# Moving the two copies of a head's row maxima from SP's DMA queue to ACT's

## The reference

```
q, k, v = x @ Wq, x @ Wk, x @ Wv          # 16 query heads of 32; layer 0: 4 key heads with rope
att = einsum('bhqd,bhkd->bhqk', q, k) / sqrt(32)
att = softmax(where(causal, att, -inf))
y   = einsum('bhqk,bhkd->bhqd', att, v)
x   = x + y @ Wo
```

## Time and profile before

| | |
|---|---|
| median of 3 runs | 2565.97 us (2558.61 to 2567.2) |
| time of the profiled execution | 2561.6 us |
| its span | 2559.9 us |
| mean granted TensorE clock | 0.993 |
| PE busy | 96% of the span |
| DVE, ACT, POOL busy | 68%, 50%, 59% |
| chain that ended last | PE 81%, DVE 6%, POOL 3%, ACT 2%, issue 2%, DMA 1%, SP's queue 1% |

### The profile page before, as it was taken

One profiled execution on the slowest core, in us unless ns is written; L12 is line 12 of the kernel. 1 busy time (PEld: TensorE's weight loads), 2 busy tenths in 40 slices (PEclk: granted clock), 3 DMA queues, 4 the chain that ended last, 5 costly groups with the idle time before them and its releaser, 6 DMA issues.

```text
span 2559.9 us, 45686 instructions
## 1 busy us (share of the span) xinstructions
PE 2451.0 (96%) x16544; PEld 1938.2 (76%) x16544; DVE 1751.9 (68%) x3608; ACT 1285.7 (50%) x2521; POOL 1509.2 (59%) x2045
## 2 busy tenths in 40 slices
PE   6999989999999999899999999999999889999999
PEld 4788767676768888688888888776777578888887
DVE  7788579979976344756565555788588866565555
ACT  6555346646664223554555443566466645454443
POOL 5433567667662334876677643666456876676662
PEclk9999999999999999999999999999999999999999
DMA  4222032122221110111111113233233211111112
GB/s 152 74 75 71 33 82 52 47 68 56 56 57 50 38 54 1 39 61 50 50 50 50 50 41 75 72 89 73 53 89 86 58 54 50 50 50 56 59 60 74
DMA packets 85840, 154.01 MB, mean 60 GB/s; under 512 B 17264, under 2 KB 26480, under 8 KB 85616
## 3 DMA queue, kind: packets, MB, share of 16 engines
q1 hardware_dynamic: 85616, 151.09, 20.5%
HBM read 87.58 MB, written 13.63 MB: 40 GB/s over the span
## 4 chain that ended last, share of the span: by engine, by line
PE 81%; DVE 6%; POOL 3%; ACT 2%; issue 2%; DMA 1%; SPq 1%; DVEq 0%; POOLq 0%; ACTq 0%
PE psum L1393 41%; PE psum L1444 23%; PE psum L1539 5%; PE psum L1502 5%; PE psum L1520 4%; PE psum L1550 2%; DVE psum L1972 2%; PE psum L1402 1%; ACT s4a1e L1757 1%; DVE s1a0rden L2011 1%; SPq L2251 1%; POOL s1a0e L2166 1%; ACT s1a0e L1757 1%; POOL s4a1e L2166 0%; POOL x L2174 0%
## 5 line engine op out<-in xcount | busy, mean ns | idle before, releaser
L1972 DVE CUSTOM_DVE_ANT_0 psum<-psum,mask_q 128x512 f32<-128x512 f32 (+5 forms) x768 | 413.1, 574 | 97.8 <-PE psum L1502 94.8
L1925 DVE SCALAR_TENSOR_TENSOR x<-psum,x 128x512 f32<-128x512 f32 x256 | 176.7, 691 | 289.6 <-PE psum L1393 289.2
L1757 ACT ACTIVATE s4a1e<-psum,p_scale 128x384 f32<-128x384 f32 (+5 forms) x384 | 206.1, 580 | 93.2 <-PE psum L1520 89.6
L1757 ACT ACTIVATE s1a0e<-psum,p_scale 128x384 f32<-128x384 f32 (+5 forms) x384 | 202.4, 578 | 79.7 <-PE psum L1520 78.3
L1393 PE MATMUL psum<-s5f1wd,s5f1a 128*128 128x512 f32 x768 | 196.7, 393 | 3.0 <-DVE s5f1a L1917 2.2
L1444 PE MATMUL psum<-s3f1h,wmem 128*128 128x512 f32 x768 | 195.3, 397 | 3.4 <-DVE s3f1h L1886 2.2
L1393 PE MATMUL psum<-s3f1wd,s3f1a 128*128 128x512 f32 x768 | 198.1, 393 | 0.3 <-issue 0.3
L1444 PE MATMUL psum<-s5f1h,wmem 128*128 128x512 f32 x768 | 192.6, 394 | 0.0
L2166 POOL TENSOR_TENSOR s4a1e<-s4a1e 128x896 f32<-128x896 f32 (+3 forms) x128 | 164.8, 1287 | 17.5 <-ACT s4a1e L1757 6.6
L2166 POOL TENSOR_TENSOR s1a0e<-s1a0e 128x896 f32<-128x896 f32 (+3 forms) x128 | 164.5, 1285 | 17.1 <-ACT s1a0e L1757 5.8
L1444 PEld LDWEIGHTS psum<-s3f1h,wmem 128*128 128x128 f32 x768 | 143.4, 188 | 38.0 <-issue 4.6
(11 more groups left out here) (233 smaller groups left out, 6186.5 us busy)
## 6 DMA issues: line engine op xcount, KB each, us to landing
raw<-in_down SPq DMA_DIRECT2D x76, 256.0 KB, 3.9
s1a0qst<-s1a0qs SPq DMA_DIRECT2D x96, 128.0 KB, 2.4
s4a1qst<-s4a1qs SPq DMA_DIRECT2D x96, 128.0 KB, 2.4
s4a1kst<-s4a1ks SPq DMA_DIRECT2D x96, 128.0 KB, 2.4
s3f1graw<-in_gate SPq DMA_DIRECT2D x32, 256.0 KB, 3.0
s3f1graw<-in_up SPq DMA_DIRECT2D x32, 256.0 KB, 3.1
s5f1graw<-in_gate SPq DMA_DIRECT2D x32, 256.0 KB, 3.0
s5f1graw<-in_up SPq DMA_DIRECT2D x32, 256.0 KB, 3.0
```

What stands on the lines that cost most here:

```text
L1757: act.activation(T[s]["e32"][:, begin_ + z * pw:begin_ + (z + 1) * pw - skip], src, ACT.Exp, bias=p_scale[:]).then_inc(sem["exp"], 1)
L1925: dve.scalar_tensor_tensor(x[:, tile, :], src, 0.5, x[:, tile, :], ALU.mult, ALU.add).then_inc(sem["x_add"], 1)
L1972: dve.tensor_tensor_reduce(scores, scores, mask_q[:, first:first + pw], -1.0, -MASKED, ALU.add, ALU.min, T[s]["negmax"][n % 2][:, column:c ...
```

## The change

The function that waits for the two parts and issues the two copies is taken out of SP's program and put into ACT's, under the same step (`m_lo`) of the same plan. The plan, the tiles, the semaphores and the copies themselves stay as they are; PSUM banks too.

```diff
 in scalar_program:
+            def m_move(s, n):
+                t, j = T[s], n % HPG
+                ready = (("m_hi", "m_hi"), ("m_lo", "m_lo"))
+                for p, (name, kind) in enumerate(ready):
+                    dst = t["qst"][STACK + p:STACK + p + 1, j, :].bitcast(F32)
+                    on.wait_ge(sem[name], at(name, kind, s, n))
+                    act.dma_start(dst.rearrange("o (i q) -> o i q", q=P),
+                                 t["mrow"][n % 2][p][:].bitcast(F32)).then_inc(m_in[n % 2], 16)
...
-                     "key": key, "y_hi": y_hi}
+                     "key": key, "y_hi": y_hi, "m_lo": m_move}
 in sync_program:
-            def m_lo(s, n):
-                t, j = T[s], n % HPG
-                ready = (("m_hi", "m_hi"), ("m_lo", "m_lo"))
-                for p, (name, kind) in enumerate(ready):
-                    dst = t["qst"][STACK + p:STACK + p + 1, j, :].bitcast(F32)
-                    on.wait_ge(sem[name], at(name, kind, s, n))
-                    sp.dma_start(dst.rearrange("o (i q) -> o i q", q=P),
-                                 t["mrow"][n % 2][p][:].bitcast(F32)).then_inc(m_in[n % 2], 16)
...
-                     "w_back": w_back, "stack": stack, "m_lo": m_lo}
+                     "w_back": w_back, "stack": stack}
```

## The result

| | before | after |
|---|---|---|
| median of 20 runs each | 2564.53 us (2558.61 to 2572.96) | 2570.96 us (2566.96 to 2577.53) |
| ratio of after to before | | 1.0027, interval 1.0017 to 1.0037 |
| time of the profiled execution | 2561.6 us | 2576.6 us |
| its span | 2559.9 us | 2574.9 us |
| mean granted TensorE clock | 0.993 | 0.988 |

A forecast was written before the change was run, and what follows sets the result against it. PE was taken to bound the kernel, busy 96% of the span and 81% of the chain. Terms +14.5 + 1.5 - 4.0 = +12 us on the median 2565.97 gave 2578 us, range 2562 to 2596.

The forecast's parts named there:

- the likeliest case: Both runs of heads: ACT issues of 0.65 us overlapping the running exp, net +6 to +18 us; chance 0.45.
- The walk through the heads: All 64 heads: each delayed exp followed to the matmul taking its bank; 17 heads lose 0.3 to 1.5 us, sum 14.5.
- The copies were hidden already: In 45 of 64 heads SP already waited for `m_hi`, so copies mostly begin no earlier; head 16's landed 0.6 us early.
- the faster rival: SP's queue: earlier stacks, weights and `y` copies remove most DMA waits, 4.9 - 13 = -8 us, 2558; chance 0.07.
- The rival in series: ACT's queue: each issue waits until the running exp is over, +26 us, 2592; chance 0.18.
- the rival of a very short issue: ACT's issue takes 0.1 to 0.3 us, or PE's idle time or existing waits cover losses: +1 us, 2567; chance 0.27.
- The second exp 0.84 us late in head 16: Head 16 of a0: the 384-column exp starts behind the second issue, 0.84 us late; PE loses about 0.07 us.
- Sum of PE's loss: PE waiting for late exps: 14.5 us over 64 heads, 4.9 with 0.1 us issues, 27 with 0.9 us.
- meeting SP: ACT issues beside SP's in 19 of 64 heads: 1.5 us taken, bounds nothing to 4 us.
- SP gives back 4 us: a1, heads 3 and 23: earlier copy and output weight shorten PE's waits, 4 us taken, range 0 to 6.
- The mutual holding: ACT and SP issuers hold each other: 0.9 us and more per issue, in series, over +35 us; chance 0.03.
- PE's idle time grows by 15 us: Profile sign: PE's waits for ACT's exps grow in both attentions by about 15 us.

The follow-up runs named there:

- SP held back: The kernel after, with SP still waiting for DVE's low part as before and issuing nothing there: 2573.60 us, 1.0026 of the kernel before.
- the wait alone: The kernel before, with ACT also waiting for DVE's low part and issuing nothing, SP keeping both copies: 2564.76 us, 1.0003 of the kernel before.
- twice the issues: The kernel after, with a second 4 KB DMA to unread DRAM scratch behind each copy on ACT: 2616.11 us, 1.0190 of the kernel before.
- the early output weight: The kernel before, with the output weight's load put three units earlier on SP: 2564.11 us, 0.9990; once more 2563.40 us, 0.9990.

## Why the prediction was right, and what was mis-sized

The forecast was 2578 us with 2562 to 2596; 2570.96 lies inside that range, just below the likeliest case's own 2572 to 2584. The mechanism came out as it was told, in the part of its chance (0.12 of 0.45) that was to stay below +0.3%; the size is little more than half of the forecast. The walk through the heads is on record in two of them only, 16 and 27, so its sums can be held against measured totals but not redone head by head. The range's upper end, 2596, is not the sum that is named for it: 28.6 and 4 us give 2599, and 2595 with SP's 4 us taken off. Point by point:

- *The copies were hidden already; they do not begin earlier to any use.* Right. Both copies on ACT without the late exp are worth 1.3 us (0.9995, one that its interval does not tell from nothing), and the first alone 3, not the 13 that the faster rival needed; SP held back changes nothing.
- *Issue of 0.65 us, overlapped with the running exp.* Right: 0.627 us, starting 0.01 us after the exp. The rival in series (2592) is out by this start, the rival of a very short issue by the duration.
- *The second exp 0.84 us late in head 16, PE's 1.4 us in head 27.* 0.87 and 1.40. A third place, in a1, shows a wait of the same kind, on the same line as head 27's:

```profile
1746.27 0.95 PE L1393 MATMUL psum<-s4a1ow,s4a1yT 128*128 128x512 f32 x3 [1.31 <-ACT s4a1e L1757]
```

- *Sum of PE's loss, 14.5 us, and 1.5 for meeting SP.* This is the mis-sized term. By the ratios the second copy costs 10.8 us alone, 10.0 on top of the first (6.9 and 3.1), and 8.2 against the kernel that issues it one exp later (6.9 and 1.3): 8 to 11 us instead of 16. The 1.5 us for meeting SP should have been near nothing (below), which leaves 14.5 against 8 to 11. In the profiled executions the term looks larger: head 0 to head 31 of both attentions, the change, its repeat and SP held back lie 13.8 us above the two executions with the first copy alone. So the ratios say that the walk's sum was too large, while the profiles nearly bear the walk out; the size stays open between 8 and 14 us. Whether idle time that PE has anyway takes up part of each head's lateness, which the walk did not count, no run here shows.
- *SP gives back 4 us.* The size is near in one kernel, 3.0 and 3.7 us by the medians for the first copy alone (where SP keeps one copy and its wait), and not in the one that frees SP of both (1.3); the working was not. For head 3 of a1 two waits were counted, 1.4 for `mrow` and 1.1 behind the output weight. PE's timeline of the kernel after, and SP's:

```profile
1636.09 0.70 PE L1520 MATMUL psum<-s4a1qst,s4a1kst 98*128 98x512 f32 x2 [0.22 <-DMA s4a1qst<-s4a1mrow]
...
1639.35 1.08 PE L1539 MATMUL psum<-s4a1e,s4a1v 128*32 128x256 f32 x8 [2.02 <-ACT s4a1e L1757]
```

```profile
1634.62 0.61 SPq L2227 DMA_DIRECT2D raw<-in_o  x1
```

  The first wait fell from 1.68 to 0.22, as forecast. The weight went out 4.00 us after the start of `m_hi` (1630.62) where it had been 5.36 (1626.70, with `m_hi` at 1621.34): 1.36 earlier, forecast 1.37. But PE's wait behind it rose from 1.08 to 2.02, for PE now comes there sooner. It passes that point 8.73 us after `m_hi` instead of 9.81, a gain of 1.08 in all. Two waits in a row for one late queue are one gain here, not two. And the gain does not last: the lag falls by 1.0 us at the first `key` matmul of head 3 and rises by 2.5 by that of head 4, in the repeat too (0.9 and 2.5). A new wait for an exp (0.95 us, before a pair of L1502 matmuls) stands ahead of the first of these two points; between them the granted clock is 0.50 for 10.2 us from 1638.4, where before it was 0.50 for 6.8 us from 1627.9. Where the first-copy kernel's 3 us come from was not located.
- *ACT issues meeting SP's.* Where SP issued in a row from 1629.98 to 1639.11, with pauses of 0.05 us, ACT's queue in the kernel after shows:

```profile
1632.74 0.66 ACTq L1774 DMA_DIRECT2D s4a1qst<-s4a1mrow  x1
...
1633.44 0.64 ACTq L1774 DMA_DIRECT2D s4a1qst<-s4a1mrow  x1
```

  0.03 and 0.01 us over the minimum. Of the 128 issues 34 lie beside one of SP's; without the first of all they take 0.634 us in the mean, the others 0.631. The mutual holding is out, and the 1.5 us for it should have been near nothing. The one issue over 0.72 us is the first of a0, 1.22 us, beside two of SP's; but the first one on ACT is just as long, 1.22 to 1.23, in the kernels with one copy on ACT, with the second later and with SP held back, where no SP issue lies beside it, so it is no meeting. The Trainium skill ("Perfetto Trace Analysis", section "DMA Instruction — HWDGE (DVE, Sync)") puts the wait for a shared generator's lock inside the recorded duration; no such wait of more than 0.03 us shows in the two rows above, and none of over 0.1 us in any other issue of this trace but the first.
- *PE's idle time grows by 15 us.* Wrong as a sign to look for, though the loss was there: 5.8 us of waits for exps, and 13.7 us more of busy time. Part of that is waiting of weight loads that PE's own record does not show, as in head 16. Another part is the clock. In the trace's record of the granted clock, without the stretch in which the span ends, the kernel before stood at 0.50 (1.2 GHz) in 9 stretches, 37.5 us together, the kernel after in 13, 58.0 us. 20.5 us more at half speed are at most 10 us of work lost, of the pair's 15. The other kernels: 44.4 us with the first copy, 68.3 with the second, 44.4 with the wait alone, 44.4 with the second copy later, 58.0 with SP held back, 51.2 in the repeat of after, 95.6 with twice the issues. That goes with the losses, but the early output weight has 58.0 us and, with the second copy later as well, 68.3, and neither is slower than before. So the clock is not the whole of it, and how much of the loss comes by way of it no run separates. Why the profiled pair lies further apart than the medians stays open.

## What to carry to other kernels

A DMA issue on ACT's queue ran here beside the instruction before it and in front of the one behind it. It was free where it followed a longer exp and had nothing to wait for, and it made the next exp late by its wait and its length where it had to wait with work queued behind, so look at each issue's place, not at their sum. When several waits hang on one late queue, follow the chain through them: in the one place that was followed the gain was near that of one of them, not the total. A busy share can hide waiting, so check the start times of the same instruction in both traces before you believe that an engine "worked longer".

## What the hardware showed beyond that

**A small copy that landed late.** In head 6 of a0 in the kernel after, the chain shows

```profile
409.25 4.23 DMA s1a0qst<-s1a0mrow
```

where it was 1.77 us at head 0 of the kernel before and 2.04 at head 0 of this one, and SP was issuing at the same moment:

```profile
408.24 0.58 SPq L2227 DMA_DIRECT2D raw<-in_q  x1
...
408.92 1.96 SPq L2260 DMA_DIRECT2D s1a0qst<-s1a0qs  x3
```

Most of the copies' 512-byte pieces had ended by 411.45; the last began at 412.79. One 16 KB packet of the queue that loads instructions ran from 410.65 to 411.94 meanwhile. It does not explain the landing by itself: such a packet, 0.90 to 1.25 us long, stands near the same place in every other kernel that was run, also in the kernel before (409.11, 0.99 us) and in the repeat of after, where the copy is in time. With SP held back the copy was late at the same head again (4.53 us), and PE lost 2.01 us there; with only the second copy on ACT it lost 2.47. In four more kernels it lost 0.4 to 0.9 us at this head, and in two of these the second copy was SP's. So the late landing belongs to no one issuing queue, and what makes it is open. The Trainium skill ("DMA: Bandwidth & Descriptors", section "Issuing engines are not separate DMA queues") says that transfers of all issuing engines run on the same 16 engines and interleave, and that a second issuer saves only the time of the issuing. The trace agrees as far as it goes: a late landing came with either issuer.

**The clock behind such a wait.** PE's timeline behind that landing, and the windows before and after it (busy us of PE, PEld, DVE, ACT and POOL, granted clock, DMA share, GB/s):

```profile
413.62 1.19 PE L1520 MATMUL psum<-s1a0qst,s1a0kst 98*128 98x512 f32 x2 [1.70 <-DMA s1a0qst<-s1a0mrow]
```

```profile
400.00:411.90 11.90, 11.73 (x159) 8.08 (x157) 11.02 (x35) 8.05 (x17) 8.06 (x13) 1.00 0.23 61
413.00:419.80 6.80, 6.18 (x33) 3.56 (x34) 4.58 (x12) 2.94 (x5) 3.25 (x6) 0.50 0.07 18
```

PE was busy 11.73 of 11.90 us at full clock (2.4 GHz) and then idle for 1.70 us, from 411.92. From 413.0, 1.1 us into that wait, the granted clock was 0.50 (1.2 GHz) until 419.80; its pair of 512-column matmuls took 1.19 us, where the same pair in the kernel before took 0.63. 6.80 us at half speed are up to 3.4 us of work lost, twice the wait itself, and no row of waits shows them. Behind the waits of 2.01 and 2.47 us at the same head in the two other kernels the clock was 0.50 too, for 6.8 us from 415.7 and for 3.4 us from 418.4.
